# Scale and shift on GpSimd, two-pass chunk sums, in-place score maxima, other first and last stages

## The reference, cut to what matters

```python
mod = (silu(c) @ wmod).reshape(8, 6, 1, -1)          # sa, ca, ga, sb, cb, gb per batch
h = layernorm(x) * (1 + ca) + sa
# mixer: z/xBC/dt = h @ W_in1.T; causal conv of 4 taps over xBC; PReLU
#   A_t = softplus(dt) * -exp(A_log); chunked SSD: exp of cumulative sums of A_t
#   u2 = gelu(h @ W_in2.T); hn = layernorm(u2 * Y) * ln_g + ln_b; out = hn @ W_in3.T
x = x + ga * mixer(h)
h = layernorm(x) * (1 + cb) + sb                      # <- scale and shift
h2 = h + attention(rmsnorm(h, g1))                    # 16 heads of 8, causal, rope
y = h2 + moe(rmsnorm(h2, g2))                         # 8 experts, top 2, hidden 384
x = x + gb * y
```

## Time and profile before

| what | value |
|---|---|
| median of 3 runs | 476.73 us (475.59 to 480.74) |
| profiled execution | 474.64 us, of which the span of instructions is 472.9 |
| busy PE / PEld / DVE / ACT / POOL | 81 / 63 / 66 / 51 / 45% of the span |
| mean granted TensorE clock | 0.875 of full |
| XB loads, issue to landing | 1.8 us median |
| YL loads, issue to landing | 3.8 to 6.6 us, first issue at 458.22 |
| stages | first stage to 43.8 us, loop to 348, MoE to 458, end to 472.9 |

### The profile page before, as it was taken

The page is one execution under the profiler, slowest core; times in us unless marked ns, Lnnn a source line. Parts: engine busy times, 40 slices in busy tenths (PEclk is TensorE's granted clock), DMA queues, the critical chain, the costliest instruction groups (busy, mean ns, idle before and its releaser), DMA issues. The chain is left out here.

```text
span 472.9 us, 9431 instructions
## 1 busy us (share of the span) xinstructions
PE 383.0 (81%) x2798; PEld 296.5 (63%) x2798; DVE 313.7 (66%) x1255; ACT 242.4 (51%) x600; POOL 215.1 (45%) x253
## 2 busy tenths in 40 slices
PE   1796898697999999999898887856528899999940
PEld 1455777474768777777575654634313799999930
DVE  3523499987979899998969576478250455545416
ACT  1175643472767858587664737755210445545510
POOL 1111335443454774757564352656430169644430
PEclk9998799997999999999968696755658999999985
DMA  8300000000201102030120552002041112212116
GB/s 300 122 0 2 0 1 0 3 0 2 94 1 37 60 25 94 15 104 14 34 74 23 199 186 93 20 6 95 23 154 47 29 49 61 73 49 59 34 56 236
DMA packets 20993, 29.24 MB, mean 62 GB/s; under 512 B 2322, under 2 KB 17816, under 8 KB 20560
## 3 DMA queue, kind: packets, MB, share of 16 engines
q1 hardware_dynamic: 18240, 21.59, 13.9%
q0 software_dynamic: 2272, 4.43, 2.8%
q10 hardware_dynamic: 432, 2.62, 1.6%
HBM read 14.38 MB, written 14.25 MB: 61 GB/s over the span
## 5 line engine op out<-in xcount | busy, mean ns | idle before, releaser
L1385 DVE CUSTOM_DVE_ANT_0 JUNK<-bank,PACK 128x128 f32<-128x128 f32 (+1 forms) x256 | 74.2, 352 | 14.5 <-PE bank L927 14.5
L1743 POOL DMA_INDIRECT rows_by_token<-YB,IDX x39 | 38.1, 977 | 54.5 <-DVE YB L1849 50.1
L1169 ACT ACTIVATE PT<-bank 128x512 f32<-128x512 f32 x96 | 51.6, 617 | 17.3 <-PE bank L959 17.3
L1582 POOL TENSOR_SCALAR_AFFINE_SELECT PT<-PT 128x512 f32<-128x512 f32 x64 | 41.8, 671 | 20.1 <-ACT PT L1169 19.6
L289 POOL DMA_INDIRECT rows_by_expert<-XR,POS x32 | 32.0, 1001 | 16.5 <-POOLq L565 8.4
L800 PE MATMUL bank<-HTH,VH 128*128 128x256 f32 x96 | 31.9, 333 | 3.9 <-issue 3.9
L1863 DVE TENSOR_TENSOR GU<-bank,SG 128x384 f32<-128x384 f32 x39 | 21.7, 557 | 18.5 <-ACT SG L1788 14.5
L927 PE MATMUL bank<-KT,QT 32*128 32x128 f32 (+1 forms) x256 | 28.9, 327 | 5.4 <-DVE MX L1385 3.0
L1939 PE MATMUL bank<-WD,GUT 128*128 x234 | 32.6, 276 | 0.6 <-DVE YB L1849 0.6
L1919 PE MATMUL bank<-EARLY_H,XH 128*128 x78 | 29.6, 380 | 2.7 <-DVE XL L1832 2.1
L927 PEld LDWEIGHTS bank<-KT,QT 32*128 32x128 f32 x256 | 19.6, 201 | 19.1 <-DVE MX L1385 12.0
(11 more groups left out here) (246 smaller groups left out, 1047.6 us busy)
## 6 DMA issues: line engine op xcount, KB each, us to landing
rows_by_expert<-EMPTY SPq DMA_DIRECT2D x8, 1040.0 KB, 5.5
XB<-rows_by_expert SPq DMA_DIRECT2D x39, 65.0 KB, 1.8
CW<-in_convw SPq DMA_DIRECT2D x4, 576.0 KB, 10.6
YL<-rows_by_token SPq DMA_DIRECT2D x4, 512.0 KB, 5.2
RAW<-in_wg SPq DMA_DIRECT2D x1, 1536.0 KB, 7.0
RAW<-in_wu SPq DMA_DIRECT2D x1, 1536.0 KB, 11.7
WD<-in_wd ACTq DMA_DIRECT2D x1, 1536.0 KB, 7.2
X<-in_x ACTq DMA_DIRECT2D x2, 512.0 KB, 7.1
```

The costliest lines, as they stand in the source:

```text
L1169: nc.scalar.activation(to, of, ACT.Exp, scale=AD ** -0.5).then_inc(p_ev.sem, 1)
L1385: last = nc.vector.tensor_tensor_reduce(out=JUNK[:, n % 2, i * w:(i + 1) * w], in0=BANK[f"s{n}"][:, i * w:(i + 1) * w], in1=MASK[:, 256 - ...
L1582: nc.gpsimd.affine_select(out=block, in_=block, compare_op=ALU.is_ge, fill=0.0, base=0, pattern=[[0, NG], [1, 128]], channel_multiplier=-1 ...
L1743: nc.gpsimd.indirect_dma_start(out=yt, out_offset=bass.IndirectOffsetOnAxis(ap=IDX[c % NX][:, j:j + 1], axis=0), in_=YB[i % NYB][:], in_of ...
```

## The change

Scale and shift become a step `b_x2` of GpSimd: `Bx2-13` leaves VectorE's table, `Bx2-3` stands in GpSimd's behind `Ag1`. DA is split once into two fp32r tiles (three small VectorE operations), `a_g` makes two tiles per chunk instead of one, and `b_seg` sums them with two fp32r matmuls. The maximum's masked scores are written back to the bank that they come from; JUNK and the wait that guarded it are gone. The first stage's list, the MoE stage's beginning and the end are put in another order, and at the end GpSimd and a second DMA queue take a part.

```diff
                     def modulate(b):
-                        if b < 2:
-                            pe.wait_ge(v_lo, b + 1)
-                        else:
+                        if b in (4, 5):
+                            pe.wait_ge(v_lo, b - 3)
+                        elif b >= 2:
                             pe.wait_ge(mb_ev, b - 1)
...
+                    for b in range(4):
+                        modulate(b)
+                    pe.wait_ge(mod_col, 2)
+                    pe.wait_ge(in_pack[1], DMA)
                     fold(0)
                     fold(1)
                     turned(0, 0)
                     for g in range(NGRP - 2):
                         turned(g + 1, (g + 1) % 2)
-                        modulate(2 * g)
-                        modulate(2 * g + 1)
+                        modulate(4 + 2 * g)
+                        modulate(4 + 2 * g + 1)
                         group(g, g % 2)
                     turned(NGRP - 1, 1)
-                    for b in range(4, B):
-                        modulate(b)
                     fold(2)
+                    fold(3)
                     group(NGRP - 2, 0)
                     group(NGRP - 1, 1)
-                    fold(3)
...
-                           "Cs6-14 Cs7-14 Cwo-15 Bx2-13 Cs8-14 Dve-15 Cs9-14 Bsq-13",
+                           "Cs6-14 Cs7-14 Cwo-15 Cs8-14 Dve-15 Cs9-14 Bsq-13",
...
-                            "Bseg0-1 Dsc2-6 Dsc3-6 Ag1 Dpw-5 Bsq-3 Bseg1-1 Bsplit-3 Bsplit1-3 E0-4 E1-4 E2-4 "
+                            "Bseg0-1 Dsc2-6 Dsc3-6 Ag1 Bx2-3 Dpw-5 Bsq-3 Bseg1-1 Bsplit-3 Bsplit1-3 E0-4 E1-4 "
...
-                            pe.matmul(BANK[f"seg{t}"][:], UP, G[t][:].rearrange("p h l -> p (h l)"),
-                                      start=True, stop=True).then_inc(seg_ps.sem, 1)
+                            pe.matmul(BANK[f"seg{t}"][:], UP_R[:], GH[t][:].rearrange("p h l -> p (h l)"),
+                                      start=True, stop=False)
+                            pe.matmul(BANK[f"seg{t}"][:], UP_R[:], GL[t][:].rearrange("p h l -> p (h l)"),
+                                      start=False, stop=True).then_inc(seg_ps.sem, 1)
...
-                            need(dve, s_max.sem, s_max.at(b, n - 1))
                             apart(dve, parted)
                             for i, g in enumerate(gs):
                                 last = nc.vector.tensor_tensor_reduce(
-                                    out=JUNK[:, n % 2, i * w:(i + 1) * w],
+                                    out=BANK[f"s{n}"][:, i * w:(i + 1) * w],
...
-                            nc.gpsimd.tensor_tensor(
-                                G[t][:], TRI.unsqueeze(1).to_broadcast([128, NH, 128]),
...
+                            for to, of in ((GH, DAH), (GL, DAL)):
+                                last = nc.gpsimd.tensor_tensor(
+                                    to[t][:], TRI.unsqueeze(1).to_broadcast([128, NH, 128]),
...
+                    def b_x2(b, p):
+                        scale, shift = (MB[:, steps_of(b, 1), m, :].to_broadcast([128, T, D])
+                                        for m in (CBM, SBM))
+                        if b == 0:
+                            need(pool, mod_fix, 2 + 6 * (B // 2))
+                        need(pool, x1.sem, x1.at(b, 6))
+                        nc.gpsimd.tensor_tensor(GO[:], GO[:], scale, ALU.mult).then_inc(x1.sem, 1)
+                        need(pool, x1.sem, x1.at(b, 7))
+                        need(pool, h2_done.sem, h2_done.at(b - 2, 1))
+                        nc.gpsimd.tensor_tensor(HX[p][:], GO[:], shift, ALU.add).then_inc(x1.sem, 1)
...
-                need(pe, in_wd, DMA)
-                need(pe, tbl_exp, 1)
                 for i in range(WARM_UP):
                     pe.matmul(P[2 + i % 2][:], IDENT, PACK[0][:, 0:512], start=True, stop=True)
+                need(pe, tbl_exp, 1)
                 turn(0, 0)
+                turn(0, 1)
                 need(pe, w_lo, 2 * E)
                 expert = {}
                 for i in range(NBLK):
                     c, j = i // CHK, i % CHK
                     expert[i] = gate_up(i)
-                    if i < CHK - 1:
-                        turn(0, i + 1)
+                    if i < CHK - 2:
+                        turn(0, i + 2)
...
-                for g in range(B // 2):
+                for g in (0, 2):
                     sp.dma_start(YL[g][:], by_token[:, 4 * g:4 * g + 4]).then_inc(yl_in[g], DMA)
-                for g in range(B // 2):
+                for g in (0, 2, 1, 3):
                     sp.wait_ge(fin[g], 3)
...
+                for g in (1, 3):
+                    act.dma_start(YL[g][:], by_token[:, 4 * g:4 * g + 4]).then_inc(yl_in[g], DMA)
```

More of the change, by code:

```diff
@@ L589, in adaln_block @@
                 CBS = ms("CBS", [128, T, 128])
-                G = [ms(f"DAT{t}", [128, NH, 128]) for t in range(T)]
+                GH = [ms(f"DATH{t}", [128, NH, 128], R) for t in range(T)]
+                GL = [ms(f"DATL{t}", [128, NH, 128], R) for t in range(T)]
+                DAH, DAL = ms("DAH", [128, B * T, NH], R), ms("DAL", [128, B * T, NH], R)
+                UP_R = ms("UP_R", [128, 128], R)
+                da_split = main.enter_context(nc.semaphore("da_split"))
                 EL = [ms(f"EL{t}", [128, NH, 128]) for t in range(T)]
@@ L1482, in signed @@
                             need(dve, mod_fix, n + 3 * i + 2)
-                            nc.vector.scalar_tensor_tensor(out=MB[:, now, m, :], in0=SIGN[:], scalar=-1.0,
+                            nc.vector.scalar_tensor_tensor(out=MB[:, now, m, :], in0=SIGN, scalar=-1.0,
                                                            in1=MAG[:], op0=ALU.add, op1=ALU.mult
@@ L1793, in _ @@
                 turned(NBLK - 1)
+                for k in range(NYB):
+                    need(act, y_out[k], DMA * len(range(k, NBLK, NYB)))
+                by_token = yt.rearrange("(n p c) d -> p n c d", p=128, c=2)
+                for g in (1, 3):
+                    act.dma_start(YL[g][:], by_token[:, 4 * g:4 * g + 4]).then_inc(yl_in[g], DMA)
             @block.vector
```

94 lines of the change are left out of this document (53 added, 41 removed), and 2 rows, old and new, of the table ORDER.

## The result

The changed kernel takes 490.54 us (median of 3 runs, 490.01 to 491.05) against 476.73: ratio 1.027, interval 1.020 to 1.035. (Ratios leave out runs in a slower state of the chip, so they are not always the quotient of the medians.) The forecast was 474 with a range to 484, so it is slower where I expected no change or a little less. The profiled execution is 490.01 us (span 488.2), 15.3 above that of before in span.

| stretch | before | after | forecast | measured |
|---|---|---|---|---|
| first stage, to the last matmul of TensorE's list | 41.5 | 36.4 | -4.5 | -5.1 |
| loop, from there to the count matmul | 306.5 | 330.6 | +9.0 | **+24.1** |
| MoE stage, count matmul to first YL issue | 110.2 | 104.9 | -6.7 | -5.3 |
| end, first YL issue to the end of the span | 14.7 | 16.3 | +1.5 | +1.6 |

The account below looks back on a forecast made before the run. TensorE and VectorE were taken as nearly full in the loop, with GpSimd having room. From 474.64, the terms -4.5, +0.3, +8.7 (loop), -6.7 and +1.5 gave 473.9, forecast 474 us, range 463.5 to 484.

Parts of the forecast that it names:

- First stage: Before the loop: four modulations fill TensorE's wait for weights, and the stage ends near 38.1 instead of 42.60, -4.5 us.
- MoE start: Start of the MoE stage: warm-up begins at 348.6, but loads set the second chunk's turn, so -6.7 us, not 8.
- end: Last additions: two load queues and three operations on GpSimd, between no gain and 3.1 us later, middle taken, +1.5 us.
- rival 2: Loop: new stalls of 2.8 us in rounds 3, 6 and 7 bring TensorE's clock to half; 482 us, chance 0.16.
- Bound: -2.6 to +2.6 us; I take 0: Loop: the 256 maxima writing to PSUM change by at most 10 ns each, judged from CBS and HX; 0 taken.
- Chunk sums: Loop: two fp32r matmuls replace one fp32, saving some 0.3 us each; four places of 0.4 counted, -1.6 us.
- Ag0 ... is hidden: Loop, GpSimd: the doubled Ag0 multiply lies before a 1.93 us wait for EL and costs nothing.
- I charge nothing for it: Loop: GpSimd holding VectorE off, as with the shift's 1.38 us, priced at zero because VectorE is mostly waiting then.
- Rival 3: Loop: GpSimd's added SBUF operations hold VectorE off, 0.96 us once a round in eight rounds, +7.7; 481.6 us, chance 0.10.
- Scale and shift: Loop: moved to GpSimd behind Ag1, they make HX late and with it the round's end; sum over rounds +10.3 us.
- 7.25 against 7.4: Sign in round 6 of the loop: HX on GpSimd would end about 7.4 us after EL's start instead of 3.3.
- round 3, priced at 3.4: Loop, round 3: HX behind the doubled Ag1 puts VER at 98.2 instead of 94.81, +3.4 us.

Follow-up runs that it names:

- back_three: The changed kernel with all three loop changes taken back (shift on VectorE, one-pass sums, masked scores into the SBUF tile): 468.19 us, ratio 0.983.
- stages_no_end: The changed kernel with the loop changes and the end taken back, leaving only the new first stage and MoE start: 466.32 us, ratio 0.976.
- only_max: The kernel before with one change, masked scores written back to their PSUM bank, JUNK and its wait gone: 490.96 us, ratio 1.022.
- back_x2_seg: The changed kernel with scale and shift on VectorE and one-pass chunk sums, only the in-place maxima left in the loop: 480.37 us, ratio 1.007.
- back_x2: The changed kernel with scale and shift back on VectorE at their old place, all else kept: 488.25 us, ratio 1.026.
- x2_best: The kernel with new first stage and MoE start alone, plus scale and shift on GpSimd right behind the first EL multiply: 477.89 us, ratio 0.999.

## Why the prediction was wrong

- *Which bound.* "Both leading engines are nearly full and a wait of 2 us in both is lost time" was right, but it is lost twice: once as a wait and, where the clock falls, once more as half clock behind it.
- *First stage, MoE start, end.* -5.1, -5.3 and +1.6 against -4.5, -6.7 and +1.5. Right, and back_three and stages_no_end confirm the sum: 0.976 to 0.983 of the kernel before. In the MoE start the loads were issued 9.4 us behind the count matmul instead of 8.8; the low clock that rival 2 named for that stretch came as well (0.61 from 380 to 384), but there the loads set the time.
- *The step that failed most: "Bound: -2.6 to +2.6 us; I take 0" for the in-place maxima.* They cost 10 to 12 us (only_max, back_x2_seg against back_three). The bound came from an operation that reads PSUM against one that reads SBUF, and both write SBUF; no row had one that writes to PSUM, and I took the nearest as if it were near. A term without a row, 256 times over, deserved a wide range: at 10 per cent of 352 ns each it is 9 us.
- *Chunk sums: "I take 0.4 x 4 = -1.6 us" and "Ag0 ... is hidden".* TensorE's gain per sum is real (0.3 us), but the pair of GpSimd operations cost 6 to 13 us. I priced the doubled Ag1 as a delay of HX alone. It delays the router's root as well, which stands behind it in GpSimd's list, and with it XR. And the row that I had read, VectorE's shift held for 1.38, showed another way: "I charge nothing for it" was a mistake, since VED held 1.88 us delays MN. Rival 3 had that mechanism at 0.10; the run that shows both is back_x2, where HX is not late.
- *Scale and shift: +10.3.* In round 6 the place was right to 0.15 us (7.25 against 7.4) and the wait too, and the waits for HX added in all are 9.4 us. That the whole comes near +10.3 is in part luck: round 3, priced at 3.4, had a wait of 0.79. Its price is 0.4 to 3 us when taken out of the changed kernel, 7 when put into the kernel before, 11 in x2_best: probably other waits cover it where they stand beside it.
- *The clock (rival 2, 0.16).* It happened as described, after all three long waits (in rounds 6, 7 and 8, not 3, 6 and 7), and not only after waits of 2.8 us: it came behind 0.77 and 0.76 us close together in back_x2, and behind 0.57 in only_max. It should have been the main case. Whether the falls cause all of what the tally puts beside them stays open: fillers brought back about 4 us in the changed kernel (1.027 to 1.018), about 7 in the one with in-place maxima (1.007 to 0.993, from three runs) and nothing in back_three.
